# Last turn of a cross-attention loop: output weights loaded earlier, four value banks, output products by tile, one set of statistics for two layernorms

## Reference

```python
x = x + cross_attention(layernorm(x), ctx)      # 16 heads, latent keys = values = rotated ctx
x = x + self_attention(layernorm(x))            # its first line is a layernorm again, then scale, shift, W_in
x = x + ffn(layernorm(x))                       # activations quantised to 8 bits, weights to -1, 0, 1

# inside cross_attention, behind the softmax:
ctx_c   = einsum('bhsl,bld->bhsd', attn, kv_r)       # per head 256 x 128
ctx_lat = einsum('bhsd,hkd->bhsk', ctx_c, w_kc_kv)   # "value product"
out     = ctx_lat.reshape(B, S, 16 * 128) @ Wo.T     # "output product", 16 heads summed
```

## Time and profile before

| | us |
|---|---|
| median of 3 runs (558.12 to 559.95) | 558.31 |
| the profiled execution | 559.53 |
| its span, first to last instruction | 557.7 |
| PE busy | 529.8 (95%) |
| VectorE busy | 454.9 (82%) |
| ScalarE busy | 365.7 (66%) |

### The profile page before, as it was taken

The page is one execution under the profiler, slowest core; times in us unless marked ns, Lnnn a source line. Parts: engine busy times, 40 slices in busy tenths (PEclk is TensorE's granted clock), DMA queues, the critical chain, the costliest instruction groups (busy, mean ns, idle before and its releaser), DMA issues.

```text
span 557.7 us, 10036 instructions
## 1 busy us (share of the span) xinstructions
PE 529.8 (95%) x3831; PEld 355.1 (64%) x3835; DVE 454.9 (82%) x660; ACT 365.7 (66%) x447; POOL 148.6 (27%) x202
## 2 busy tenths in 40 slices
PE   6989998799999999999999999999997998998996
PEld 3767763367667666676676676676676785555543
DVE  3444986999999999999999999999995547478686
ACT  2134436886886886886886886886886344986442
POOL 2467863002202202202202202202000001596500
PEclk9999999899999999999999999999997999999999
DMA  8999287699999999999999999999998997600000
GB/s 304 353 356 306 95 151 229 113 200 198 190 197 211 202 197 197 213 212 204 204 191 207 204 195 203 198 201 203 203 188 168 218 431 297 259 1 1 2 1 38
DMA packets 288350, 107.93 MB, mean 194 GB/s; under 512 B 276928, under 2 KB 278464, under 8 KB 286912
## 3 DMA queue, kind: packets, MB, share of 16 engines
q1 hardware_dynamic: 288320, 107.54, 88.7%
HBM read 37.79 MB, written 0.52 MB: 69 GB/s over the span
## 4 chain that ended last, share of the span: by engine, by line
PE 73%; DVE 11%; ACT 6%; DMA 5%; issue 3%; SPq 1%; ACTq 0%; DVEq 0%
PE ps L669 18%; PE ps L671 9%; PE ps L651 9%; PE ps L652 9%; PE ps L653 9%; PE ps L700 4%; PE ps L711 3%; DVE rows L1281 2%; DMA pT<-split 2%; DMA keys<-ctxT 2%; ACT junk L1071 2%; PE ps L722 2%; DVE split L1262 1%; PE ps L883 1%; PE ps L619 1%
## 5 line engine op out<-in xcount | busy, mean ns | idle before, releaser
L669 PE MATMUL ps<-pT,VH 128*128 128x256 f16 x1024 | 197.4, 274 | 0.5 <-DMA pT<-split 0.4
L671 PE MATMUL ps<-pT,VL 128*128 128x128 f16 x1024 | 183.9, 220 | 0.0
L1281 DVE TENSOR_SCALAR_CACHE_REDUCE rows<-ps,qback 128x1024 f32<-128x1024 f32 x128 | 163.7, 1280 | 17.8 <-PE ps L653 17.4
L1040 ACT ACTIVATE split<-rows,rz 128x2048 f16<-128x2048 f32 x64 | 124.8, 1994 | 67.7 <-DVE rz L1228 65.6
L1262 DVE SCALAR_TENSOR_TENSOR split<-rows,rz,split 128x2048 f16<-128x2048 f32 x64 | 150.3, 2350 | 0.8 <-issue 0.7
L1026 ACT ACTIVATE rows<-rows,negm 128x2048 f32<-128x2048 f32 x64 | 127.2, 1988 | 0.2 <-DVE negm L1286 0.2
L669 PEld LDWEIGHTS ps<-pT,VH 128*128 128x128 f16 x1024 | 100.9, 99 | 40.4 <-DMA pT<-split 2.0
L671 PEld LDWEIGHTS ps<-pT,VL 128*128 128x128 f16 x1024 | 100.8, 98 | 28.3 <-issue 0.7
L532 POOL TENSOR_TENSOR ctx_c<-acc 128x128 f32<-128x128 f32 x32 | 23.8, 744 | 298.5 <-ACT acc L1015 298.5
L651 PE MATMUL ps<-KH,qcur 128*128 128x512 f16 x256 | 97.5, 381 | 3.3 <-DVE rows L1281 3.3
L652 PE MATMUL ps<-KL,qcur 128*128 128x512 f16 x256 | 97.5, 381 | 0.0
(11 more groups left out here) (176 smaller groups left out, 630.2 us busy)
## 6 DMA issues: line engine op xcount, KB each, us to landing
w_sb<-w SPq DMA_DIRECT2D x3, 2816.0 KB, 15.8
wq_sb<-wq SPq DMA_DIRECT2D x4, 1024.0 KB, 8.0
wo_sb<-wo SPq DMA_DIRECT2D x16, 256.0 KB, 4.7
wkcq_sb<-wkcq SPq DMA_DIRECT2D x4, 768.0 KB, 9.7
keys<-ctxT SPq DMA_DIRECT2D x8, 256.0 KB, 8.5
stage<-ctxT SPq DMA_DIRECT2D x16, 128.0 KB, 8.9
stage<-kcos SPq DMA_DIRECT2D x8, 256.0 KB, 9.1
stage<-ksin SPq DMA_DIRECT2D x8, 256.0 KB, 9.6
```

Of the source, the lines that this page charges most:

```text
L669: nc.tensor.matmul(bank(6 + r % 2, 0, 256), VH[:, 4 * b + k, :], p.rearrange("p x q -> p (x q)"), start=(b == 0 and k == 0), stop=False)
L671: last = nc.tensor.matmul(bank(6 + r % 2, 0, 128), VL[:, 4 * b + k, :], p[:, 0, :], start=False, stop=(b == 7 and k == 3))
L1040: nc.scalar.activation(split[:, split_slot(r, half), :, 0, :], rows[:, k, half * 2048:(half + 1) * 2048].rearrange("p (b k) -> p b k", k=1 ...
L1281: nc.vector.tensor_scalar(rows[:, k, c * 1024:(c + 1) * 1024], ps[:, score_bank(s) * 512:(score_bank(s) + 2) * 512], qback[:, r // 2:r // ...
```

## The change

The second half of `wo` is loaded behind `wkv`, before the loop. Value products rotate through four PSUM banks (0, 1, 4, 5) and stand at other steps, as do the high and low parts; all sixteen heads of `wo` are split inside the last turn. VectorE makes the last row's low halves at steps 4 and 5. Behind the loop PE makes all of tile 0's output products, then tile 1's, with tile 0's `z1` transposes ahead of the last three of these. One `bn_stats` of `x_sb` serves both layernorms: the second variance is `v / (v + eps)`, so `z1 = (x - mean) / sqrt(v (1 + eps) + eps^2)`; `z1` is written before `h1`. New tiles `ve2`, `sd2`, `rs2`, `nt2` and semaphores are left out below, as is the renumbering of later waits.

```diff
-    SPLIT_STEPS = (12, 14, 16, 17, 18, 19, 20, 21)
-    PRODUCT_STEPS = (18, 19, 20, 21, 22, 23)
+    VALUE_STEPS = (3, 5, 9, 11, 13, 15, 17)
+    VALUE_BANK = (0, 1, 4, 5)
+    CONTEXT_STEPS = (5, 6, 7, 8, 12, 14, 18)
+    SPLIT_STEPS = (6, 7, 8, 9, 10, 11, 12, 13, 15, 16, 17, 19, 20, 21, 22, 23)
+    PRODUCT_STEPS = (15, 17, 19, 19, 21, 21)
...
@@ sync
                 sp.dma_start(wkv_sb[:, heads, :], wkv[:, heads, :]).then_inc(wkv_in, 16)
+            for h in range(XH // 2, XH):
+                sp.dma_start(wo_part(wo_sb, h), wo[:, h, :]).then_inc(wo_in[h // 4], 16)
             sp.wait_ge(qpart_done, XH)
...
             for r in range(2 * XH):
                 turn_row(r)
-            for h in range(XH // 2, XH):
-                sp.dma_start(wo_part(wo_sb, h), wo[:, h, :]).then_inc(wo_in[h // 4], 16)
             sp.wait_ge(av_done, 16 * XH)
@@ gpsimd
-                pool.wait_ge(z_done, TT + 2 * t + 1)
+                pool.wait_ge(h1_done, t + 1)
@@ tensor, value_product
-                wait(pe, ctxl_lo_done, n - 1)
+                wait(pe, ctxl_lo_done, n - 3)
                 for a in range(2):
-                    last = nc.tensor.matmul(bank(n % 2, a * TOK, (a + 1) * TOK), wkv_sb[:, 2 * n + a, :],
+                    last = nc.tensor.matmul(bank(VALUE_BANK[n % 4], a * TOK, (a + 1) * TOK), wkv_sb[:, 2 * n + a, :],
@@ tensor, attention_step
-                if last_turn(i) and s % 2 == 0 and 2 <= s < XH:
-                    value_product(s // 2 - 1)
-                if last_turn(i) and s in PRODUCT_STEPS:
-                    output_product(0, PRODUCT_STEPS.index(s))
+                if last_turn(i) and s in VALUE_STEPS:
+                    value_product(VALUE_STEPS.index(s))
+                for h in range(len(PRODUCT_STEPS)):
+                    if last_turn(i) and s == PRODUCT_STEPS[h]:
+                        output_product(0, h)
@@ tensor, behind the loop
-            for first in (0, XH // 2):
-                for t in range(TT):
-                    for h in range(len(PRODUCT_STEPS) if t == 0 and first == 0 else first, first + XH // 2):
-                        output_product(t, h)
-                        if first == 0 and t == 1 and h == 1:
-                            value_product(XH // 2 - 1)
...
+            for h in range(len(PRODUCT_STEPS), XH):
+                if h == 10:
+                    value_product(XH // 2 - 1)
+                output_product(0, h)
+            for h in range(XH):
+                if h == 13:
+                    pe.wait_ge(z1_done, 1)
+                    tile_transposes(z1[:, 0, :], 0, zT_done)
+                output_product(1, h)
...
-            pe.wait_ge(z_done, TT + 2)
-            tile_transposes(z1[:, 0, :], 0, zT_done)
             project(0, 0)
             pe.wait_ge(x1_done, TT)
             project(0, 1)
-            pe.wait_ge(z_done, TT + 4)
+            pe.wait_ge(z1_done, 2)
             tile_transposes(z1[:, 1, :], 1, zT_done)
@@ scalar, attention_step and behind the loop
-                if last_turn(i) and s % 2 == 1 and 3 <= s < XH + 1:
-                    context_high(s // 2 - 1)
+                if last_turn(i) and s in CONTEXT_STEPS:
+                    context_high(CONTEXT_STEPS.index(s))
...
             accumulator_copy(2 * XH - 1, 1)
-            for h in range(len(SPLIT_STEPS), XH):
-                if h == 10:
-                    context_high(XH // 2 - 1)
-                output_weight_high(h)
+            context_high(XH // 2 - 1)
...
+            def both_roots(t):
+
+                act.wait_ge(ve2_done, 2 * t + 2)
+                nc.scalar.activation(sd2[:, t, :], ve2[:, t, :], ACT.Sqrt).then_inc(sd_done, 1)
+
...
-            root(3, slice(0, 1))
-            root(4, slice(0, 1))
+            both_roots(0)
             scale_shift(0)
-            root(5, slice(1, 2))
+            both_roots(1)
             abs_sum(0, 0)
-            root(6, slice(1, 2))
             abs_sum(0, 1)
             natural_copy(0, 0)
             abs_sum(0, 2)
-            abs_sum(0, 3)
             natural_copy(0, 1)
             scale_shift(1)
+            abs_sum(0, 3)
             for c in range(3):
                 abs_sum(1, c)
@@ vector, attention_step
                 if s % 8 in (0, 2) and active(i, s, LOLAG):
                     row, r = row_of(i, s, LOLAG)
...
+                    if not isinstance(i, int) or row < 2 * XH - 1:
+                        row_low(row, r, s % 8 // 2)
+                if last_turn(i) and s in (4, 5):
+                    row_low(2 * XH - 1, 5, s - 4)
...
-                if last_turn(i) and s % 2 == 1 and 3 <= s < XH + 1:
-                    context_low(s // 2 - 1)
+                if last_turn(i) and s in CONTEXT_STEPS:
+                    context_low(CONTEXT_STEPS.index(s))
@@ vector, behind the loop
-            for h in range(len(SPLIT_STEPS), XH):
-                if h == 10:
-                    context_low(XH // 2 - 1)
-                output_weight_low(h)
+            context_low(XH // 2 - 1)
+
+            def two_layernorms(t):
+
+                link(nc.vector.bn_stats(st[:, t, :], x_sb[:, t, :]))
+                variances[0] += 1
+                nc.vector.bn_aggr(mv[:, t, :], st[:, t, :]).then_inc(var_done, 1)
+                dve.wait_ge(var_done, variances[0])
+                nc.vector.tensor_scalar(ve2[:, t, 0:1], mv[:, t, 1:2], EPS, None, ALU.add).then_inc(ve2_done, 1)
+                nc.vector.tensor_scalar(ve2[:, t, 1:2], mv[:, t, 1:2], 1.0 + EPS, EPS * EPS, ALU.mult, ALU.add)\
+                    .then_inc(ve2_done, 1)
+                roots[0] += 1
+                dve.wait_ge(sd_done, roots[0])
+                link(nc.vector.reciprocal(rs2[:, t, :], sd2[:, t, :]))
+                dve.wait_ge(ve2_done, 2 * t + 2)
+                link(nc.vector.tensor_tensor(nt2[:, t, :], rs2[:, t, :], ve2[:, t, :], ALU.mult))
+                link(nc.vector.tensor_tensor(nt2[:, t, :], nt2[:, t, :], rs2[:, t, :], ALU.mult))
+                link(nc.vector.tensor_scalar(nt2[:, t, :], nt2[:, t, :], -0.5, 1.5, ALU.mult, ALU.add))
+                link(nc.vector.tensor_tensor(rs2[:, t, :], rs2[:, t, :], nt2[:, t, :], ALU.mult))
+                nc.vector.tensor_scalar(z1[:, t, :], x_sb[:, t, :], mv[:, t, 0:1], rs2[:, t, 1:2],
+                                        ALU.subtract, ALU.mult).then_inc(z1_done, 1)
+                nc.vector.tensor_scalar(h1[:, t, :], x_sb[:, t, :], mv[:, t, 0:1], rs2[:, t, 0:1],
+                                        ALU.subtract, ALU.mult).then_inc(h1_done, 1)
+
             for t in range(TT):
...
-                layernorm(x_sb, h1, t, t + 1)
-                dve.wait_ge(z_done, TT + 2 * t + 1)
-                layernorm(h1, z1, t, t + 1)
+                two_layernorms(t)
```

More of the change, by code:

```diff
@@ L162, in program @@
         nt = small("nt", [128, TT])
+        ve2 = small("ve2", [128, TT, 2])
+        sd2 = small("sd2", [128, TT, 2])
+        rs2 = small("rs2", [128, TT, 2])
+        nt2 = small("nt2", [128, TT, 2])
         mx = small("mx", [128, 3, 4])
@@ L227, in program @@
         hT_ps = sem("hT_ps")
+        h1_done = sem("h1_done")
         hTn_done = sem("hTn_done")
@@ L277, in program @@
         var_done = sem("var_done")
+        ve2_done = sem("ve2_done")
+        z1_done = sem("z1_done")
         w1_in = sem("w1_in")
@@ L1000, in context_high @@
                 act.wait_ge(ctxl_ps, n + 1)
-                nc.scalar.activation(ctxl_hi[:, 2 * n:2 * n + 2, :].rearrange("p h t -> p (h t)"), bank(n % 2), ACT.Copy)\
+                nc.scalar.activation(ctxl_hi[:, 2 * n:2 * n + 2, :].rearrange("p h t -> p (h t)"), bank(VALUE_BANK[n % 4]), ACT.Copy)\
                     .then_inc(ctxl_hi_done, 1)
@@ L1138, in residual_copy @@
                 nc.scalar.activation(x_sb[:, t, :], bank(6 + t), ACT.Copy).then_inc(x3_done, 1)
-            root(7, slice(0, 1))
+            root(5, slice(0, 1))
             residual_copy(0)
@@ L1143, in _ @@
             nc.scalar.activation(h2T[:, 0, :], bank(6).bitcast(bf16)[:, 0:DM], ACT.Copy).then_inc(h2T_done, 1)
-            root(8, slice(1, 2))
+            root(6, slice(1, 2))
             residual_copy(1)
@@ L1212, in context_low @@
                 pair = slice(2 * n, 2 * n + 2)
-                nc.vector.tensor_tensor(ctxl_lo[:, pair, :].rearrange("p h t -> p (h t)"), bank(n % 2),
+                nc.vector.tensor_tensor(ctxl_lo[:, pair, :].rearrange("p h t -> p (h t)"), bank(VALUE_BANK[n % 4]),
                                         ctxl_hi[:, pair, :].rearrange("p h t -> p (h t)").bitcast(f32),
@@ L1254, in query_factor, with row_low @@
                 nc.vector.tensor_scalar(qfac[:, a:b], qrec[:, a:b], kinv[:, 0:1], None, ALU.mult).then_inc(qfac_done, 1)
+            def row_low(row, r, half):
+                k = r % 3
+                dve.wait_ge(hi_done, 2 * row + half + 1)
+                nc.vector.scalar_tensor_tensor(out=split[:, split_slot(r, half), :, 1, :],
```

(15 more changed lines are left out.)

## The result

The changed kernel takes 555.32 us (median of 9 runs, 554.70 to 557.16) where the kernel before took 559.92 beside it (9 runs, 558.12 to 561.74): ratio 0.9922, interval [0.9905, 0.9939], or 4.4 us less, where 6.5 were forecast. The three runs known before had a median of 558.31, so 1.6 us of the distance between 551.8 and 555.32 is the base and about 2 us is the change. Its profiled execution has a span of 553.36 us against 557.74.

A forecast was written before the change was run, and what follows sets the result against it. TensorE, busy 95% of the span, was taken as the bound, so only its waits and slow stretches could be won: 4.4 + 2.1 = 6.5 us off the profiled 559.53, 553.0, and 551.8 as median; range 549.0 to 555.5.

The forecast's parts named there:

- The stall, its echo and the two banks: Loop's last turn: PE idles 2.94 us on a shared PSUM bank, then runs at half clock; 5.9 us removed.
- What is late next: Loop's last turn: transposing DMAs of rows 30 and 31 become the next waits, leaving a first gain of 4.4 us.
- the four waits: PE's predicted waits on transposes: 0.4, 1.0 and 0.1 us in row 30, 0.9 us for row 31's chunk 0.
- the step count that gave 4.4: From 431.4: wait 0.9, eight steps 5.3, one value product 0.9, five output products 3.75; end 442.2 against 446.55.
- second gain 2.1: Behind the loop: PE's two waits before the transposes and first projection go, 2.33 us, less a new wait of 0.2.
- The new wait at `weight_sum(0)`: PE waits for ScalarE's fourth absolute sum of `w1`, now behind `scale_shift(1)`: 0.2 us, bounds 0 and 1.5.
- worth nothing more at PE: One set of statistics: the shorter sum-to-`z1` time is hidden by tile 1's products and two projections, so only cover.
- Everything behind 479 us is unchanged and moves as a whole: Kernel's part behind 479 us: the sum of 6.5 us won ahead of it reaches the end.
- The second rival: Projections: ScalarE's absolute sums and the late `w3` request give the second gain back; 554 to 555 us, chance 0.13.
- The moved load: Output weights' second half loaded behind `wkv`, ahead of row 0's transposes: cost taken as 0, bound 1.5 us; rival's chance 0.08.
- The transposes bind harder: Loop's end: chunks landing 1.7 us late more than once, or a 2.9 us wait; 554 to 556.5 us, chance 0.12.
- the prediction's own signs of being wrong: `pT` wait over 1.5 us, half clock in drain, first probability product after 108.8, or `weight_sum(0)` wait over 0.5 us.

The follow-up runs named there:

- two_banks: The changed kernel with value products back on two PSUM banks, each waiting for the last but one eviction; ratio to the kernel before 0.9976.
- fetch_earlier: The changed kernel with PE's instruction stream 80 instructions longer ahead of the loop, by satisfied waits in the head; ratio to the kernel before 0.9930.
- fetch_between: The changed kernel with satisfied waits put where PE already idles, in six attention steps and before the second query total; median 554.84 us, ratio 0.9915.
- both_shifts: The changed kernel with the edits of fetch_between and sums_first together; 552.73 us, ratio to the kernel before 0.9882.
- old_statistics: The changed kernel with two layernorms in a row again, each with its own statistics; 556.97 us, ratio to the kernel before 0.9950.
- scale_first: The changed kernel with VectorE making the first weight scale directly behind the first weight total; 555.34 us, ratio to the kernel before 0.9924.
- sums_first: The changed kernel with the fourth absolute sum, first weight sum and weight scale each made earlier in their queues; 553.64 us, ratio 0.9892.

## Why the prediction was wrong in size and right in kind

**The stall, its echo and the two banks: right.** No wait on `ctxl_lo`, no digit at 418 to 432 us, and two_banks brings both back.

**"What is late next" (first gain 4.4): mis-sized, 2.52.** The waits on `pT` came to 3.65 us where I had 2.4. Row 30's second transpose landed in 5.07 us, not 4.4, and PE waited 1.44, not 1.0. The packet was charged to row 31's first chunk, where PE has two products more in its way (0.9 us). It fell into row 30's last, which I had landing in time: 1.86 us. I knew that PE's stream reaches that place sooner and did not work out what it meets there: the packet moved by 4.5 us (433.82 to 429.30), the transposes around it by only 1.0 and 2.4 (426.05 to 425.02 and 429.65 to 427.25), so it met the chunk before. fetch_earlier, fetch_between and both_shifts, with the packet elsewhere, have 1.6 to 1.8 us less in b. Another 0.45 is a slip: 6.3 less the four waits is 3.9, and the step count that gave 4.4 ran short. The last 0.16 is a loop that ended later (412.20 against 412.04).

The Trainium skill, "Runtime: NRT & Kernel Launch", section "Instruction fetch mechanics", calls the cost of such a fetch "mostly hidden". For the engine that fetches, no row read here shows a wait for instructions. For a transpose in flight it isn't hidden: 6.2 us against 4.5 to land.

**Behind the loop (second gain 2.1): right, 2.64.** Both waits went (2.33 us). The new wait at `weight_sum(0)`, charged at 0.2, did not come; old_statistics shows its mechanism, with 0.71 us. There "worth nothing more at PE" failed: one set of statistics also clears ScalarE's queue, which I had counted only for the kernel as changed.

**"Everything behind 479 us is unchanged and moves as a whole": wrong, 0.78 us.** It is unchanged, but held by two chains. PE moved by 5.16 us at `weight_sum(0)` and by 5.35 at 500 us; GpSimd's chain moved by 4.38, since VectorE makes the scale that starts it 2.04 us behind `weight_sum(0)`, 1.25 before; the clip ends 1.48 us behind that chain, before and after (507.97 - 506.49, 503.59 - 502.10). scale_first and sums_first pull the chain forward and shorten d by 0.92 and 1.77 us. The second rival had a chain of weights as its mechanism, but by the absolute sums and the request for `w3`, and within the projections. There PE waited 0.55 us, at `weight_sum(1)` (481.79), and had made it up by 491 us, where the old wait of 0.69 for `qkn` is gone. GpSimd's passes were not in it.

The Trainium skill, "SBUF — State Buffer", section "Who interferes with whom", has VectorE's `tensor_scalar`, in its two-port modes, and a GpSimd instruction exclude each other for a whole instruction. The trace agrees that the clip is held (3.44 us against 1.61), and shows more: GpSimd's instructions last about 0.75 us each (eight in 5.97), and the clip of 500.15 outlasts two or three of them, to the end of the chain.

**The moved load: right, as far as can be told.** The first product with the values starts at 108.97 against 108.78, SyncE issues the last small load at 99.3, and the loop ends its scores 0.16 us later. It was taken at 0, bound 1.5; with the same head that first product starts at 108.55 to 110.06 in other profiled runs, so 0.2 us can't be told from nothing.

**The rivals.** "The transposes bind harder" came closest: one more chunk 1.7 us late. It gave 554 to 556.5; that 555.32 lies in it is owed in part to the base, 1.6 us higher than the 558.31 it was worked out from. Two of the prediction's own signs of being wrong came, a wait on `pT` over 1.5 us (1.86) and a first product with the values later than 108.8. That a wait would have to reach 2.9 us to bring the half clock is contradicted: it came behind 1.4 and 2.0 us. What decides between runs of one kernel stays open.

## What to carry to other kernels

When a stall goes, the next wait must be worked out with everything that moves with it, and the instruction packets of the engine move too: shift the last packet before the stretch by the time that the engine gains, and see whose transfer it meets, to within the 2 us by which it differs between executions here. "The rest moves as a whole" holds only if each engine's chain into the rest starts earlier by the same amount, so look for the engine that is released last (here GpSimd, by a scale standing behind a rotation and the value copies in VectorE's queue). A load that looks like a side part of a change can be what carries it, so undo it alone.

## What was not expected of the hardware

One packet of the instruction queue (0.02 MB) lengthens the landing of a transpose in flight: in the drains of the twelve profiled runs those with such a packet between issue and landing took 4.9 to 6.6 us, the others 4.2 to 5.2, and the longest was over 6 in every run but two_banks. Its place follows the number of instructions ahead of it, though not in proportion: 80 more on PE moved it from 429.3 to 424.5 (fetch_between) and 424.8 (fetch_earlier), 20 fewer to 435.3.

The granted clock fell to its half level in the drain behind two waits of about 1.4 and 2.0 us with 4.7 us of work between them (scale_first), in three of the five profiled runs that have waits of 1.3 to 1.4 and 1.9 to 2.0, and cost about 1.7 us each time (33.5 to 33.6 against 31.8 in b).

A clip of 1.61 us took 2.5 to 3.5 when it started during GpSimd's chain, and ended 1.48 us behind the chain in all ten profiled runs in which it did, whatever its start.
